# Layer normalisation cut into single VectorE instructions placed between the maxima of the scores

## The reference

```python
def _layernorm(x, axis=-1, eps=1e-05):
    m = jnp.mean(x, axis=axis, keepdims=True)
    v = jnp.var(x, axis=axis, keepdims=True)
    return (x - m) / jnp.sqrt(v + eps)
...
x = x + causal_attention(_layernorm(x))      # projections with biases, mask k <= q
x = x + split_attention(_layernorm(x))       # tokens in two classes; a query sees its own class and 5 registers
x = x + rotary_attention(_layernorm(x))      # rotary embedding of q and k, every key
x = x + split_attention(_layernorm(x))
```

## Time and profile before

| what | value |
|---|---|
| median of the runs | 5044.56 us |
| the profiled execution | 5051.34 us, span 5049.7 us |
| TensorE matmul busy | 88% of the span |
| VectorE busy | 64% |
| ScalarE busy | 50% |
| GpSimd busy | 33% |
| mean granted TensorE clock | 0.965 |

### The profile page before, as it was taken

The page is one execution under the profiler, slowest core; times in us unless marked ns, Lnnn a source line. Parts: engine busy times, 40 slices in busy tenths (PEclk is TensorE's granted clock), DMA queues, the critical chain, the costliest instruction groups (busy, mean ns, idle before and its releaser), DMA issues. The chain is left out here.

```text
span 5049.7 us, 70670 instructions
## 1 busy us (share of the span) xinstructions
PE 4459.8 (88%) x26116; PEld 1880.7 (37%) x26116; DVE 3220.1 (64%) x6578; ACT 2547.4 (50%) x3362; POOL 1655.6 (33%) x922
## 2 busy tenths in 40 slices
PE   4899999999869988999886899999999589999999
PEld 2454545455413333333332233333333223333333
DVE  4555555455447677777772766776676277777776
ACT  1444444444425555555453465556555356656555
POOL 2354554545422425344355033333333400000000
PEclk8999999999979999999998899999999889999999
DMA  5353544444323243342432342343344223333331
GB/s 152 99 153 125 148 129 145 133 132 139 97 69 102 83 112 97 94 119 87 113 93 77 83 117 93 105 122 105 95 120 118 66 71 86 86 86 91 89 91 42
DMA packets 302269, 525.23 MB, mean 104 GB/s; under 512 B 58340, under 2 KB 236136, under 8 KB 285544
## 3 DMA queue, kind: packets, MB, share of 16 engines
q1 hardware_dynamic: 259432, 485.06, 33.5%
q10 hardware_dynamic: 42496, 35.66, 2.2%
HBM read 316.97 MB, written 201.46 MB: 103 GB/s over the span
## 5 line engine op out<-in xcount | busy, mean ns | idle before, releaser
L887 DVE TENSOR_REDUCE neg_max<-scores 128x1 f32<-128x512 f32 (+3 forms) x4096 | 2486.6, 636 | 1279.1 <-PE scores L1246 746.4
L1105 ACT ACTIVATE probs<-scores_t 128x1024 f32<-128x1024 f32 (+2 forms) x2048 | 1925.7, 946 | 1571.0 <-PE scores_t L1279 1091.1
L1246 PE MATMUL scores<-k_stack,q_stack 98*128 98x512 bf16 (+4 forms) x4096 | 1435.5, 373 | 285.1 <-DVE neg_max L887 197.8
L1279 PE MATMUL scores_t<-q_stack,k_stack 100*128 100x512 bf16 (+3 forms) x4096 | 1189.3, 364 | 67.7 <-DMA q_stack<-shift_rows 66.4
L1246 PEld LDWEIGHTS scores<-k_stack,q_stack 96*128 96x128 bf16 (+1 forms) x4096 | 397.1, 97 | 1688.0 <-DVE neg_max L887 1240.2
L1300 PE MATMUL o_ps<-probs,values 128*32 128x512 f32 (+1 forms) x8192 | 1019.7, 570 | 0.3 <-ACT probs L1105 0.3
L1279 PEld LDWEIGHTS scores_t<-q_stack,k_stack 100*128 100x128 bf16 x4096 | 377.9, 99 | 389.3 <-issue 142.3
L730 POOL TENSOR_TENSOR parts<-qk_f,parts 128x1024 bf16<-128x1024 f32 x128 | 272.5, 2129 | 678.6 <-ACT parts L1148 519.5
L750 POOL TENSOR_TENSOR sim_inv<-sim_parts,minus_half 128x64 f32<-128x64 f32 x32 | 337.6, 10550 | 206.0 <-DVE sim_parts L970 206.0
L743 POOL TENSOR_TENSOR x_res<-x_res,o_bias_s 128x1024 f32<-128x1024 f32 x32 | 75.5, 2359 | 987.5 <-DMA x_res<-x_after 987.5
L701 POOL TENSOR_SCALAR var_eps<-mean_var 128x4 f32<-128x4 f32 x64 | 14.6, 229 | 1084.5 <-DVE mean_var L851 1084.5
(11 more groups left out here) (118 smaller groups left out, 4045.4 us busy)
## 6 DMA issues: line engine op xcount, KB each, us to landing
q_stack<-q_parts SPq DMA_DIRECT2D x1536, 64.0 KB, 2.7
values<-v_stage SPq DMA_DIRECT2D x64, 1024.0 KB, 4.2
values<-values SPq DMA_DIRECT2D x64, 1024.0 KB, 6.2
k_parts<-parts SPq DMA_DIRECT2D x192, 256.0 KB, 2.7
q_parts<-parts SPq DMA_DIRECT2D x192, 256.0 KB, 4.3
k_stack<-k_parts SPq DMA_DIRECT2D x256, 192.0 KB, 3.2
k_stack<-k_parts SPq DMA_DIRECT2D x256, 128.0 KB, 3.2
x_after<-x_res ACTq DMA_DIRECT2D x48, 512.0 KB, 2.9
```

Source lines behind the costliest of these rows:

```text
L887: nc.vector.tensor_reduce(neg_max[:, h % G, t:t + 1], bank[:, 0:n], AX.X, ALU.max, negate=True).then_inc(max_done.sem, 1)
L1105: nc.scalar.activation(probs[c][:, h % G, 0:n], st[i][:, 0:n], ACT.Exp).then_inc(exp_done.sem, 1)
L1246: last = nc.tensor.matmul(bank[:, 0:n], q[0:r, h, t * P:(t + 1) * P], k[0:r, h, 0:n], start=True, stop=kind != CAUSAL)
L1279: last = nc.tensor.matmul(st[i][:, off:off + L - q0], k[0:ROWS, h, kt * P:(kt + 1) * P], q[0:ROWS, h, q0:L], start=True, stop=kind != CAUSAL)
```

## The change

`statistics` and `normalise` become sequences of single pieces, and `normal` is called after each of a slot's four maxima in place of after each pair. A key (slot, t) is the place after the maximum of tile t in that slot:
- `NXT` statistics: `bn_stats` 0 to 3 after (6, 0), (6, 2), (6, 3), (7, 0); the four `bn_aggr` together after (7, 1).
- `NXT` normalise: `tensor_scalar` 0 to 3 after (8, 0), (8, 1), (8, 2), (8, 3).
- `OWN` statistics: `bn_stats` 0 to 3 after (9, 0) to (9, 3); the four `bn_aggr` after (10, 0).
- `OWN` normalise: `tensor_scalar` 0 to 3 after (11, 0) to (11, 3).

The turns stay where they were: place 0 is now after tile 1, place 1 after tile 3. `bn_stats` pieces 0 and 1 wait for the first half of turn `out`, 2 and 3 for the second. The instructions are the same in number, shape and operands.

```diff
-NXT_STATS_AT = (6, 1)
-NXT_NORMALISE_AT = (8, 0)
-X_STATS_AT = (8, 1)
-X_NORMALISE_AT = (10, 1)
+NXT_STATS_AT = {(6, 0): 0, (6, 2): 1, (6, 3): 2, (7, 0): 3, (7, 1): T}
+NXT_NORMALISE_AT = {(8, t): t for t in range(T)}
+X_STATS_AT = {(9, 0): 0, (9, 1): 1, (9, 2): 2, (9, 3): 3, (10, 0): T}
+X_NORMALISE_AT = {(11, t): t for t in range(T)}
...
-            def statistics(B, f):
-                if f == OWN:
-                    dve.wait_ge(x_loaded.sem, x_loaded.after(B, f))
+            def statistics(B, f, piece):
+                x = x_new if f == OWN else x_res
+                if piece < T:
+                    if f == NXT:
+                        dve.wait_ge(turn_free.sem, turn_free.after(B, "out", piece // 2))
+                    elif piece == 0:
+                        dve.wait_ge(x_loaded.sem, x_loaded.after(B, f))
+                    last = nc.vector.bn_stats(bn[:, piece, :], x[:, piece, :])
+                    if piece == T - 1:
+                        last.then_inc(bn_done.sem, 1)
                 else:
-                    dve.wait_ge(turn_free.sem, turn_free.after(B, "out", 1))
+                    xn_done.wait_earlier(dve, B, 1, f)
+                    dve.wait_ge(bn_done.sem, bn_done.after(B, f))
+                    for t in range(T):
+                        last = nc.vector.bn_aggr(mean_var[:, t, :], bn[:, t, :])
+                    last.then_inc(stats_done.sem, 1)
+
+            def normalise(B, f, t):
+                if t == 0:
+                    dve.wait_ge(rstd_done.sem, rstd_done.after(B, f))
+
+                    before, key = front_before(B, f)
+                    if before is not None:
+                        turn_full.wait(dve, before, key, 1)
                 x = x_new if f == OWN else x_res
+                last = nc.vector.tensor_scalar(xn[:, t, :], x[:, t, :], mean_var[:, t, 0:1],
+                                               rstd[:, t:t + 1], ALU.subtract, ALU.mult)
+                if t == T - 1:
+                    last.then_inc(xn_done.sem, 1)
...
                 for slot in range(H):
                     m = max_head(B.n, slot)
-                    for place in range(2):
-                        if m:
-                            maximum(B + m[0], m[1], 2 * place)
-                        if place and kind == SPLIT and slot == EXTRA_AT:
+                    for t in range(T):
+                        if t == T - 1 and kind == SPLIT and slot == EXTRA_AT:
                             extra_max(B)
                         if m:
-                            maximum(B + m[0], m[1], 2 * place + 1)
-                        if place and m and m[1] % G == G - 1:
+                            maximum(B + m[0], m[1], t)
+                        if t == T - 1 and m and m[1] % G == G - 1:
                             shift(B + m[0], m[1] // G)
-                        for k, off, i in turns_of(B.s, B.n, slot, place):
-                            if k in DVE_TURNS or B.n + off < 0:
-                                take_turn(B + off, k, i)
-                        normal(slot, place)
+                        if t % 2:
+                            for k, off, i in turns_of(B.s, B.n, slot, t // 2):
+                                if k in DVE_TURNS or B.n + off < 0:
+                                    take_turn(B + off, k, i)
+                        normal(slot, t)
```

More of the change, by code:

```diff
@@ L866, in register_queries, with layer_norm @@
+            def layer_norm(B, f):
+                for piece in range(T + 1):
+                    statistics(B, f, piece)
+                for t in range(T):
+                    normalise(B, f, t)
             def register_queries(B):
@@ L976, in first @@
                     for b in range(X_AHEAD):
-                        statistics(B + b, OWN)
-                        normalise(B + b, OWN)
+                        layer_norm(B + b, OWN)
                         if b < OWN_AHEAD:
@@ L991, in body, with normal @@
                 kind = STAGES[B.s]
-                def normal(slot, place):
-                    here = (slot, place)
-                    if has_next(B.s) and here == NXT_STATS_AT:
+                def normal(slot, t):
+                    here = (slot, t)
+                    if has_next(B.s) and here in NXT_STATS_AT:
                         if B.begun:
-                            statistics(B + (-1), NXT)
-                        else:
+                            statistics(B + (-1), NXT, NXT_STATS_AT[here])
+                        elif NXT_STATS_AT[here] == T:
@@ L999, in normal @@
                             bn_done.skip(dve, B + (-1), NXT)
                             stats_done.skip(dve, B + (-1), NXT)
-                    if has_next(B.s) and here == NXT_NORMALISE_AT:
+                    if has_next(B.s) and here in NXT_NORMALISE_AT:
                         if B.begun:
-                            normalise(B + (-1), NXT)
-                        else:
+                            normalise(B + (-1), NXT, NXT_NORMALISE_AT[here])
+                        elif NXT_NORMALISE_AT[here] == T - 1:
@@ L1005, in normal @@
                             xn_done.skip(dve, B + (-1), NXT)
                     if B.s == 0 and B.n + X_AHEAD < NB:
[L1007 to L1010, removed]
+                        if here in X_STATS_AT:
+                            statistics(B + X_AHEAD, OWN, X_STATS_AT[here])
+                        if here in X_NORMALISE_AT:
+                            normalise(B + X_AHEAD, OWN, X_NORMALISE_AT[here])
@@ L1034, in finish @@
                     if (k, i) == ("out", 1) and has_next(B.s):
-                        statistics(B, NXT)
-                        normalise(B, NXT)
+                        layer_norm(B, NXT)
             n_class = 0
```

17 lines of the change are left out of this document (removed).

## The result

The kernel after takes 4957.98 us (median of 4 runs, 4954.06 to 4967.34). The kernel before took 5046.64 us beside it (median of 4, 5038.67 to 5056.37). The ratio is 0.9826, 95% interval 0.9804 to 0.9849. The forecast was 4968 us. The profiled execution has a span of 4955.5 us.

A forecast was written before the change was run, and what follows sets the result against it. TensorE was taken to bound the kernel, losing time to waits for VectorE. Stage 0 (32.8 + 1.5 + 4.0), stage 1 (22.4) and stage 2 (16.5) gave 77 us off 5051.3; less 6.8 for the median, 4968 us, range 4940 to 5022.

The forecast's parts named there:

- TensorE sets the pace, and the waits behind the blocks are what can be won: Stages 0 to 3: TensorE's matmuls busy 91% to 95%; its waits for `neg_max` fall by some 60 us.
- The walk: Slot-by-slot timing of VectorE and TensorE through the bodies of stages 0 to 2, summing to 77 us won.
- The price of a piece, 0.33 us: A piece between two maxima costs VectorE 0.33 us; bounds 0.33 and its whole duration, 0.41 us.
- The walk through stage 2: Stage 2, slots 6 to 9: 1.38 us won in slot 7, 1.10 us per body left at slot 9.
- Two `bn_stats` cost nothing in slot 6: `bn_stats` 0 and 1 fall into VectorE's idle time in slot 6; without that cover, 0.33 us each.
- Stage 0, 2.73 us a body: Bodies with both parts: `NXT` wins 1.23 us, `OWN` statistics 0.85 us, `OWN` normalise 0.65 us.
- Stage 1, 1.49 us a body: 1.38 us won in slot 7 plus 0.11 us by slot 9; 22.4 us over 15 bodies.
- GpSimd's 1/sqrt has 0.25 us to spare in stage 2 and 0.9 us or more elsewhere: `rstd` is ready that long before the first `tensor_scalar` of slot 8; rival that it is late, chance 0.06, 4980 us.
- The shift DMA is hidden: Slot 8's `scores_t` comes 1.4 us earlier, but the DMA packets show 1.2 us ahead of it.
- The win is eaten later: Rival, 0.12: TensorE comes earlier to something untied, as loads, and waits; 5045 us, or 5019 with a third left.
- Shift parts meet GpSimd: Rival, 0.08: slot 13 shifts against `prepare`, 28 bodies of stages 0 and 2 lose 7.2 us each; 5169 us.
- Two-port pieces: Rival, 0.04: `OWN` pieces in slot 11 wait for a GpSimd instruction in 12 bodies; 26 us, 4994 us.

The follow-up runs named there:

- the pairs: Against the kernel after, all four kinds of pieces placed in pairs instead of singly, in the same slots; 4971.20 us, ratio 0.9851.

## Why the prediction was right, point by point

*TensorE sets the pace, and the waits behind the blocks are what can be won.* Right. Waits for maxima fell by 71.6 us, where some 60 were forecast. The walk put the win at 77 us; the medians differ by 88.7 us and the profiled executions by 94.2 us. What lies beyond the walk is 7.7 us in stage 1, 7.3 us outside the bodies and 2.9 us in stage 3, where nothing was changed. None of it was foreseen, and the last two are as large as what other kernels of this study show from one to the next. In the sum, bodies 13 to 15 of stage 0 stand at 1.33 us where the walk has 1.23 us; that is 0.3 us.

*The price of a piece, 0.33 us.* Right, and not its duration of 0.41 us: the next maximum starts 0.33 us behind it. The recorded sum of `bn_stats` on `x_res` grew from the earlier trace rows's 66.5 us to 78.2 us (mean 411 ns), since single pieces overlap nothing in the record. That growth is no work.

*The walk through stage 2.* Right to 0.13 us at every point, in the times of after: tile 3 of slot 7 at 3106.96 (walk 3106.96), `scores_t` of slot 8 at 3108.49 (3108.50), the first `tensor_scalar` at 3110.35 (3110.45), the second tile of slot 9 at 3113.26 (3113.38), the second `scores_t` of slot 9 at 3114.07 (3114.13). A body was to win 1.10 us and won 1.1 us. Of the "one near 0.4 us at the first tiles of slot 8" there are two of 0.21 us.

*Two `bn_stats` cost nothing in slot 6.* Shown from two sides, though the second moves all four pieces: the idle shrank from 0.77 us to 0.44 us and from 0.63 us to 0.29 us, and with the pieces behind slot 6 stage 2's body is back at 73.3 us. The price put on that cover, 0.33 us each, can't be read from the second side, since that kernel also waits for `rstd`: it lost 1.0 us a body in stage 2 with 0.30 us of such waits, and 1.3 us in stage 0 with 0.96 us.

*Stage 0, 2.73 us a body.* Right: 81.1 to 78.3 us. The `NXT` statistics alone give 1.2 us and the `OWN` parts alone 1.5 us (79.9 and 79.6 us).

*Stage 1, 1.49 us a body.* The term that was off. The steady bodies give about that (79.6 to 78.2 us), but the stage won 30.1 us, not 22.4. The windows over the stage's fifteen body lengths, first before, then after, show where it came from:

```profile
1551.50:2728.90 1177.40, 1055.95 (x5870) 422.28 (x5868) 814.17 (x1486) 594.32 (x734) 493.38 (x285) 0.96 0.35 99
1508.80:2656.10 1147.30, 1046.52 (x5870) 419.38 (x5868) 807.09 (x1484) 594.79 (x734) 493.41 (x285) 0.96 0.36 101
```

TensorE idles 20.7 us less, and it is busy 9.4 us less with the same 5870 matmuls. The waits for maxima fell by 22.7 us, those for the shift DMA rose by 2.5 us. The busy time has two parts. The 0.16 us by which a recorded wait is short are 2.4 us for fifteen waits. The clock was low for 96.8 us of the stage before and 83.6 us after; 13.2 us less at 1.2 GHz instead of 2.4 are 6.6 us, an estimate that takes TensorE as busy throughout. The prediction had no term for the clock. Of the 22.7 us, 4.3 belong to one body, which took 72.6 us instead of 80.0: its second shift part met no GpSimd instruction, its first was held only 0.60 us at slot 1, the 4.3 us wait at slot 2 was missing and the clock stayed high. Two other kernels bear the clock out: with the `NXT` statistics alone and with the pairs the fourteen whole bodies have 81.9 us at low clock, as before (68.3 us after), and the stage wins 22.3 and 20.5 us. Why the clock was low for less time behind waits of the same length, and why that one body escaped the hold, is not shown. The 4.1 us between stages 0 and 1 stay unexplained.

*GpSimd's 1/sqrt has 0.25 us to spare in stage 2 and 0.9 us or more elsewhere.* Right in stages 2 and 1: one more instruction of 1.04 us costs 0.9 us in each body of stage 2, and no body of stage 1 waits for it. In stage 0 it holds for all bodies but the last two. There was nothing to spare there: VectorE waited 0.17 us for `rstd` in the kernel after.

*The shift DMA is hidden.* Right in the comparison: 66.4 us of waits before, 64.5 us after. In stage 1 it was never fully hidden (17.2 us before, 19.7 us after), and less so once the holds are gone (36.0 us), as the later experiments show.

*The win is eaten later.* Not seen in this change. It is what happened to the bias moved ahead of `prepare`: its win was in good part eaten by the waits for the shift DMA.

*Shift parts meet GpSimd.* It did not come about, and its price doesn't fit one hold. In the kernel after no shift part is held in stage 0, and in stage 2 the first part is held in 14 bodies, as it had been before: 24.0 us beyond its 0.17 us in both kernels, up to 1.90 us each. That could be read in the trace before the prediction. I priced a hold by stage 1's, at a place where two GpSimd instructions follow each other and TensorE needs the maxima. At slot 13 the bodies didn't grow by a hold of 2.0 us on the second part instead of the first (stage 2) or of 0.53 us (stage 0), in the experiment with the later `prepare`. What two holds in a row would cost there is open.

*Two-port pieces.* The number held, the reading behind it did not. A piece can be held by GpSimd. In the kernel after, body 0 of stage 0, the first piece of slot 11 meets the bias addition and not `prepare`:

```profile
162.79 2.35 POOL L745 TENSOR_TENSOR x_res<-x_res,o_bias_c 128x1024 f32<-128x1024 f32 x1
...
163.88 1.41 DVE L865 TENSOR_SCALAR xn<-x_new,mean_var,rstd 128x256 f32<-128x256 f32 x1
```

The piece ends 0.15 us after GpSimd's instruction. In the kernel with the longer 1/sqrt they start closer together, and the hold is longer:

```profile
166.19 2.35 POOL L747 TENSOR_TENSOR x_res<-x_res,o_bias_c 128x1024 f32<-128x1024 f32 x1
166.31 2.39 DVE L867 TENSOR_SCALAR xn<-x_new,mean_var,rstd 128x256 f32<-128x256 f32 x1
...
169.09 0.39 PE L1255 MATMUL scores<-k_stack,q_stack 96*128 96x512 bf16 x1 [0.84 <-DVE neg_max L899]
```

I argued that none of the 256 `tensor_scalar` of before was lengthened; none of them had met a GpSimd instruction. After, one of 256 does, in body 0, and the rival had counted 12. This is what the Trainium skill says (SBUF — State Buffer, SBUF: two separate sides): of an operation of VectorE in a two-port mode and one of GpSimd, the one that starts first has the shared ports for its whole instruction, and the other waits. The traces agree in both kernels (1.41 and 2.39 us), though a 256-column `tensor_scalar` is no faster than `bn_stats` (403 and 410 ns, medians).

## What to carry to other kernels

Put small vector work where the engine idles just before the stretch in which it falls behind. Cutting a block up without such a place wins little: 8 us here for the normalise of `NXT`, against 50 us for its statistics. Before pricing a meeting of two engines, look for places where it already happens and see whether the pace-setting engine loses anything there. When an engine's chain is moved to avoid one such meeting, look through the whole body for the next one: 1 us on GpSimd freed a shift part and caught the copy into `qx`. Where a small transfer is on the path, see which large load another queue issues just ahead of it.

## What the runs showed of the hardware

- *Which instructions of VectorE are held by GpSimd.* Behind a 2.1 to 2.35 us GpSimd `tensor_tensor` of 1024 columns, the 16-column CAST from SBUF took up to 2.15 us, the 16-column two-input operation up to 2.33 us (0.17 us each when alone), the 128-column copy from `q_stack` into `qx` up to 1.72 us (0.18 us alone) and the 256-column `tensor_scalar` 1.41 and 2.39 us (0.40 us alone). Operations that read PSUM were not lengthened: the maxima at 0.69 us, the copy of the shift rows at 0.20 us, `att` at 0.42 us. Four `bn_stats` in a run took their usual 1.39 us beside one, at the start of the kernel.
- *GpSimd's small-tile similarity instruction held no shift part.* Its 10.56 us similarity instruction of 64 columns ran beside 56 shift parts in the kernel after, and each took its 0.17 or 0.18 us.
- *A small DMA stands behind a large one on another queue.* The shift DMA, issued 0.2 us after a 1 MB load, kept TensorE waiting 2.91 us. With the load moved the wait at that slot was gone and stage 1's bodies were 2.0 us shorter on average.
